# Cross attention of a decoder layer: half of the exponentials' transposes move from TensorE to DMA, the row sums into a ones column, relu into PSUM

## The reference

```
x = x + self_attention(layernorm(x))      # over groups of 4 rows at each position, 16 heads
x = x + cross_attention(layernorm(x), ctx)   # ctx: 4 x 128 x 512, 16 heads of 32
x = x + ffn(layernorm(x))                 # see below

# cross attention, per row of the batch
scores = (q @ k.T) / sqrt(32);  scores = where(mask, scores, -1e8)
attn   = softmax(scores) ;      out = attn @ v ;  out @ Wo.T + bo

# ffn
s = x @ Win + bin                         # 64 values per token
h = relu(s[..., None] * W1 + b1)          # 16 hinges per value
g = (h * W2).sum(-1) + b2
out = g @ Wout + bout
```

## Time and profile before

| | us |
|---|---|
| median of 3 runs (lowest, highest) | 1784.15 (1783.41, 1785.06) |
| the profiled execution | 1784.44 |
| its span, first to last instruction | 1782.6 |
| TensorE busy | 1685.4 (95%) |
| VectorE busy | 1514.8 (85%) |
| ScalarE busy | 1069.8 (60%) |
| GpSimd busy | 1017.6 (57%) |
| mean granted TensorE clock | 0.983 |

### The profile page before, as it was taken

The page is one execution under the profiler, slowest core; times in us unless marked ns, Lnnn a source line. Parts: engine busy times, 40 slices in busy tenths (PEclk is TensorE's granted clock), DMA queues, the critical chain, the costliest instruction groups (busy, mean ns, idle before and its releaser), DMA issues.

```text
span 1782.6 us, 37666 instructions
## 1 busy us (share of the span) xinstructions
PE 1685.4 (95%) x13824; PEld 1392.6 (78%) x13824; DVE 1514.8 (85%) x2089; ACT 1069.8 (60%) x3420; POOL 1017.6 (57%) x721
## 2 busy tenths in 40 slices
PE   6899999999999999997799999999999999999996
PEld 5678888888888888885677787778777787777874
DVE  6788888888888888787678898888988899888886
ACT  4434444444443334442767788777877788777884
POOL 3267766666666666695554464545654465544521
PEclk9999999999999999998799999999999999999998
DMA  5410111111111111044201112011111112011101
GB/s 210 128 42 25 47 48 48 47 47 47 47 47 47 47 47 47 2 107 79 68 8 51 62 62 63 25 62 62 63 38 43 62 62 69 19 62 62 39 20 54
DMA packets 72793, 98.75 MB, mean 55 GB/s; under 512 B 22208, under 2 KB 30528, under 8 KB 72640
## 3 DMA queue, kind: packets, MB, share of 16 engines
q1 hardware_dynamic: 72064, 96.63, 17.0%
q10 hardware_dynamic: 576, 0.07, 0.0%
HBM read 59.66 MB, written 37.03 MB: 54 GB/s over the span
## 4 chain that ended last, share of the span: by engine, by line
PE 28%; ACT 12%; DVE 8%; issue 4%; DVEq 0%; POOL 0%; ACTq 0%; POOLq 0%
PE ring L1464 11%; ACT prob_c L1679 10%; DVE g_sb L1794 5%; PE sc L1492 5%; PE ring L1504 3%; PE ring L1469 3%; PE ring L1549 3%; PE sc L1484 2%; PE sc L1464 1%; DVE q_first L1975 1%; ACT relu L1660 1%; DVE g_sb L1791 1%; DVE gT L1803 1%; ACT gT L1669 1%; ACT pT L1648 0%
## 5 line engine op out<-in xcount | busy, mean ns | idle before, releaser
L447 PE MATMUL qb<-wqkv,xT 128*128 128x512 f32 x2304 | 551.9, 393 | 6.1 <-DVE wqkv L1016 6.1
L447 PEld LDWEIGHTS qb<-wqkv,xT 128*128 128x128 f32 x2304 | 429.7, 189 | 93.7 <-DVE wqkv L1016 6.3
L1679 ACT ACTIVATE prob_c<-sc,ntop 128x128 f32<-128x128 f32 x1024 | 362.6, 390 | 22.1 <-DVE ntop L1821 18.7
L1410 POOL TENSOR_TENSOR rstd<-vare,half_c 128x1 f32<-128x1 f32 x64 | 35.1, 549 | 433.6 <-DVE vare L1875 433.6
L1679 ACT ACTIVATION_READ_ACCUMULATOR prob_c<-sc,ntop 128x1 f32 x1024 | 236.1, 231 | 0.0
L352 POOL TENSOR_TENSOR prod_pool<-v,prob 128x1024 f32<-128x1024 f32 x64 | 179.9, 2810 | 67.8 <-DVE prob L911 62.6
L1464 PE MATMUL ring<-wqkv,aT_c 128*128 128x512 f32 x768 | 194.5, 402 | 8.0 <-DVE aT_c L1778 7.1
L663 ACT ACTIVATE v<-qb 128x512 f32<-128x512 f32 x64 | 38.3, 598 | 259.9 <-PE qb L447 249.6
L583 PE MATMUL ob<-wout,aT 128*128 128x512 f32 x768 | 191.4, 398 | 0.8 <-DVE aT L941 0.8
L1821 DVE TENSOR_REDUCE ntop<-sc 128x4 f32<-128x512 f32 x256 | 173.3, 683 | 12.3 <-PE sc L1492 9.5
L663 ACT ACTIVATE qk<-qb 128x512 f32<-128x512 f32 x128 | 76.1, 595 | 175.8 <-PE qb L447 175.8
(11 more groups left out here) (152 smaller groups left out, 3358.5 us busy)
## 6 DMA issues: line engine op xcount, KB each, us to landing
x_tile<-in_x SPq DMA_DIRECT2D x16, 1024.0 KB, 5.2
x_scratch<-xres SPq DMA_DIRECT2D x16, 1024.0 KB, 4.6
x_tile<-x_scratch SPq DMA_DIRECT2D x16, 1024.0 KB, 5.3
out<-x SPq DMA_DIRECT2D x64, 256.0 KB, 2.0
kt<-k_scratch SPq DMA_DIRECT2D x16, 512.0 KB, 3.2
v_c<-v_scratch SPq DMA_DIRECT2D x16, 256.0 KB, 3.6
raw<-in_wqkv SPq DMA_DIRECT2D x3, 1024.0 KB, 8.9
ctx<-in_ctx SPq DMA_DIRECT2D x1, 1024.0 KB, 8.3
```

What stands on the lines that cost most here:

```text
L447: last = nc.tensor.matmul(qb[g % 4][:, :], xT[p][a][:, k, t * P:(t + 1) * P], wqkv[b][:, k, c * D:(c + 1) * D], start=(n == 0), stop=(n == ...
L1679: last = nc.scalar.activation(prob[:, h, :], sc[g][:, (h % 4) * C:(h % 4 + 1) * C], ACT.Exp, bias=ntop[:, h:h + 1], accum_out=total[:, t % ...
```

## The change

- Tiles 2 and 3 of each step are no longer transposed on TensorE. ScalarE copies the exponentials of eight heads to float16 (`part_hi`), GpSimd (tile 2) or VectorE (tile 3) writes the low part (`part_lo`), both in SBUF, and SP issues four transposing DMAs of 128 x 1024 float16 per tile (`turn`), from `p16` to `pT`. values waits for the eight heads of each half.
- The values have 34 columns per head instead of 32: a 33rd of ones in the high part, zero in the low part, and a 34th unused. The value matmuls have 33 columns, so the sum of a row comes out beside its values. The accumulator and `total` of this stage go. The result takes two ring banks.
- The ring has places of two banks for values, and one place is skipped where two would run over the end.
- relu writes into free `sc` banks (2, 3, 1; in the last two steps 2, 3) instead of SBUF buffers.
- `aT` and the pair of `g_sb` lie in unused columns of the weights' tensor. `pT` has two pairs.
- Orders: TensorE, ScalarE, VectorE, GpSimd and SP as below.

```diff
@@ slot_turns
     if t < 3:
-        return [("aT", t)] + late + [("out", t), ("wo", t), ("pv", t), ("x2T", t), ("pT", 4 * t), ("pT", 4 * t + 1)]
+        return ([("aT", t)] + late + [("out", t), ("wo", t), ("pv", t), ("x2T", t)]
+                + ([("pT", 4), ("pT", 5)] if t == 1 else []))
+    return ([("aT", 3), ("xT", 0), ("out", 3), ("xT", 1), ("wo", 3), ("xT", 2), ("xT", 3), ("pv", 3), ("x2T", 3)]
+            + [("q", m) for m in range(DK)])
+def relu_banks(n):
+    return (2, 3) if n >= TILES - 2 else (2, 3, 1)
+def ring_places():
+    place, user, n = {}, {}, 0
+    for turn in RING:
+        width = 2 if turn[1] == "pv" else 1
+        if n % 4 + width > 4:
+            n += 1
+        place[turn] = n
+        for at in range(n, n + width):
+            user[at] = turn
+        n += width
+    return place, user
@@ SP
+            def turn(j, t, part):
+                m = 2 * j + t - 2
+                heads = slice(8 * part, 8 * part + 8)
+                for h in range(2):
+                    if h == 0:
+                        wait(sp, p_hi, 2 * m + part + 1)
+                    else:
+                        wait(sp, p_lo[t - 2], 2 * j + part + 1)
+                    wait(sp, psum["pv"], 4 * j + t - 1)
+                    sp.dma_start_transpose(pT[t % 2][h][:, heads, :],
+                                           p16[h][:, heads, :].rearrange("p h c -> p (h c)")).then_inc(turned[part], 16)
             def step(j, p):
                 # load of the next x
-                if active(j - 1, "out", 3):
-                    store(j - 1, 1 - p, 3)
                 for t in range(R - 1):
                     if active(j, "out", t):
                         store(j, p, t)
+                turn(j, 2, 0); turn(j, 2, 1)
                 if has(j, 1):
                     load_ctx(j + 1, 1 - p)
+                store(j, p, 3)
+                turn(j, 3, 0); turn(j, 3, 1)
@@ GpSimd
+                def part_lo(t, part):
+                    wait(pool, p_hi, 2 * m + part + 1)
+                    wait(pool, turned[part], 32 * m)
+                    nc.gpsimd.tensor_tensor(p16[1][:, heads, :], prob[:, heads, :], p16[0][:, heads, :],
+                                            ALU.subtract).then_inc(p_lo[t - 2], 1)
...
                     residual(0)
                     residual(1)
+                part_lo(2, 0)
+                part_lo(2, 1)
                 norm2(j, 3)
@@ TensorE
 scores:
-                        wait(pe, relu_done, PAIRS * (j - 1))
+                        wait(pe, hinged, PAIRS * (j - 1))
 values:
+                        if n_dma is not None and h % 8 == 0:
+                            wait(pe, turned[h // 8], 32 * (n_dma + 1))
-                            last = nc.tensor.matmul(dst[:, head], pT[a][:, h, :], v[:, pp, b, head],
+                            last = nc.tensor.matmul(dst[:, head // 8, head % 8, :], pT[n % 2][a][:, h, :],
+                                                    v[:, pp, b, head, 0:DH + 1],
 order:
                     values(t)
                     norm2_T(t)
-                    prob_T(4 * t)
-                    prob_T(4 * t + 1)
+                    if t == 1:
+                        prob_T(4)
+                        prob_T(5)
                 scores(3)
                 attn_T(3)
                 norm_T(0)
-                prob_T(10)
-                prob_T(11)
+                ffn_out(3)
+                norm_T(1)
                 out_proj(3)
-                norm_T(1)
-                ffn_out(3)
-                values(3)
                 norm_T(2)
                 norm_T(3)
-                prob_T(12)
-                prob_T(13)
+                values(3)
                 ffn_in(j - 1)
                 norm2_T(3)
                 for m in range(DK):
                     queries(m)
-                prob_T(14)
-                prob_T(15)
@@ ScalarE
 exps:
+                    elif t == 3:
+                        wait(act, p_lo[0], 2 * j + g // 2 + 1)
+                    else:
+                        wait(act, p_lo[1], 2 * (j - 1) + g // 2 + 1)
                     for h in range(4 * g, 4 * g + 4):
                         last = nc.scalar.activation(prob[:, h, :], sc[g][:, (h % 4) * C:(h % 4 + 1) * C],
-                                                    ACT.Exp, bias=ntop[:, h:h + 1],
-                                                    accum_out=total[:, t % 2, head_of(h):head_of(h) + 1])
+                                                    ACT.Exp, bias=ntop[:, h:h + 1])
+                def part_hi(t, part):
+                    wait(act, exped, 16 * j + 4 * t + 2 * part + 2)
+                    wait(act, turned[part], 32 * m)
+                    nc.scalar.activation(p16[0][:, heads, :], prob[:, heads, :], ACT.Copy).then_inc(p_hi, 1)
 hinges:
-                        nc.scalar.activation(relu[:, i % 4, :], sc[number][:, :], ACT.Relu, bias=hinge[:, 1, i:i + 1],
+                        nc.scalar.activation(sc[banks[i % len(banks)]][:, :], sc[number][:, :], ACT.Relu,
 order of tile 3 (part_hi(2, 0) stands behind exps(2, 1)):
+                norm2_hi(2)
+                part_hi(2, 1)
+                attn_hi(3)
+                exps(3, 0)
+                norm_hi(0)
+                exps(3, 1)
+                part_hi(3, 0)
+                norm_hi(1)
+                exps(3, 2)
+                exps(3, 3)
                 norm_hi(2)
                 norm_hi(3)
-                prob_hi(j, 12)
-                prob_hi(j, 13)
+                part_hi(3, 1)
@@ VectorE
 order of tile 3:
+                norm2_lo(2)
+                tops(3, 0)
+                attn_lo(3)
+                tops(3, 1)
+                norm_lo(0)
+                tops(3, 2)
+                add_out(3)
+                tops(3, 3)
+                norm_lo(1)
+                part_lo(3, 0)
+                add_attn(3)
+                statistics(3)
                 norm_lo(2)
                 norm_lo(3)
-                prob_lo(j, 12)
-                prob_lo(j, 13)
+                normalise(3)
+                part_lo(3, 1)
```

More of the change, by code:

```diff
@@ L1223 @@
 RING = [(j, kind, i) for j in range(TILES) for kind, i in TURNS
-        if active(j, kind, i) and (j, kind, i) not in ENDING] + ENDING
-PLACE = {turn: n for n, turn in enumerate(RING)}
+        if (j, kind, i) not in ENDING] + ENDING
+def ring_places():
[9 more added lines that the diff above has]
+    return place, user
+PLACE, USER = ring_places()
 def bank_of(j, turn):
@@ L1235, in head_of, with banks_before @@
     return 4 * (slot % 4) + slot // 4
[L1238 to L1247, removed]
+def banks_before(j, turn):
+    first = PLACE[(j, *turn)]
+    found = []
+    for at in range(first, first + (2 if turn[0] == "pv" else 1)):
+        at -= 4
+        while at >= 0 and (at not in USER or not active(*USER[at])):
+            at -= 4
+        if at >= 0 and USER[at] not in found:
+            found.append(USER[at])
+    return [(kind, TURNS_OVER[kind](step, i)) for step, kind, i in found]
+CROSS_SMALL = [("kt", [P, 2, DK, C], F32R), ("fillrows", [P, C], F32R), ("v_c", [C, 2, 2, H, VW], F16),
                ("bo", [P, D], F32), ("bf", [P, D], F32), ("hinge", [P, 3, PAIRS], F32), ("bin", [P, 1], F32),
@@ L1372, in step @@
                         store(j, p, t)
+                if has(j):
+                    turn(j, 2, 0)
+                    turn(j, 2, 1)
                 if has(j, 1):
                     load_ctx(j + 1, 1 - p)
+                if active(j, "out", 3):
+                    store(j, p, 3)
+                if has(j):
+                    turn(j, 3, 0)
+                    turn(j, 3, 1)
             for p in range(2):
@@ L1379, in _ @@
             run_steps(sp, step, TILES + 1)
-            store(TILES + 1, 1, 3)
             for p in range(2):
@@ L1401, in residual @@
                     nc.gpsimd.tensor_tensor(xr[(j + 1) % 2][:, i, :], x1[:, i, :], bo[:, :], ALU.add).then_inc(res_done, 1)
+                def part_lo(t, part):
+                    if not has(j):
+                        return
+                    m = 2 * j + t - 2
+                    heads = slice(8 * part, 8 * part + 8)
+                    wait(pool, p_hi, 2 * m + part + 1)
+                    wait(pool, turned[part], 32 * m)
+                    nc.gpsimd.tensor_tensor(p16[1][:, heads, :], prob[:, heads, :], p16[0][:, heads, :],
+                                            ALU.subtract).then_inc(p_lo[t - 2], 1)
                 def norm2(j, t):
@@ L1453, in bank @@
             def bank(j, turn):
-                before = bank_before(j, turn)
-                if before:
-                    wait(pe, taken[before[0]], before[1])
+                for kind, over in banks_before(j, turn):
+                    wait(pe, taken[kind], over)
                 return ring[bank_of(j, turn)]
@@ L1734, in step @@
                     exps(0, g)
-                for t in (1, 2, 3):
+                for t in (1, 2):
                     norm2_hi(t - 1)
```

(16 more changed lines are left out.)

148 lines of the change are left out of this document (76 added, 72 removed).

## The result

The changed kernel takes 1788.87 us (median of 14 runs, 1786.14 to 1791.95), the one before 1783.70 beside it (14 runs, 1781.92 to 1785.29): ratio 1.003, interval 1.0021 to 1.0038. It is slower by 0.3%; 1756 was forecast. One of the twelve executions of the run with the ones column alone (further down) took 3279 us and is in no comparison.

What follows compares the result with a forecast made beforehand. It took TensorE's blocks and ScalarE's exponentials in turn as the bound. Gains A 0.75, B 0.15, C 0.42 in 16 steps (21.1 us), D 0.56 in 15 (8.4), last step minus 1: 28.5 off 1784.44, so 1756; range 1736 to 1815.

Steps and rivals of the forecast that it cites:

- A: Section from scores(0) to scores(1), 8.87 us before: TensorE's own work ends last at 8.1, gain 0.75 per step.
- B: Section from scores(1) to scores(2), 9.90 us before: prob_T(5) follows normalise(1), ending at 9.75, gain 0.15 per step.
- C: Section from scores(2) to scores(3), 9.92 us before: four exponentials of 0.27 follow tops(2,3), 9.5, gain 0.42 per step.
- D: Section from scores(3) to the next scores(0), 28.31 us before: 10.4 + 17.35 = 27.75, gain 0.56 in 15 steps.
- last step behind scores(3): End of the last step: values(0) follows part_lo(3,1) and its DMA, landed about 16.5 against 15.4 before: minus 1.
- D, values(3): values(3) waits for VectorE's add_attn(3) behind part_lo(3,0) of 1.8 us: it starts 10.4 after scores(3), against 7.97 before.
- D, what follows values(3): TensorE from values(3) on: 1.25 us, then 3.23 from ffn_in to the queries, then 11.3 of queries.
- D, the tail: From the queries' end to the next scores(0): hinges start at 15.4, end with the queries; 1.55 us, 2.37 before.
- GpSimd, SP and the DMAs: GpSimd's part_lo 2.6 us each; each transposing DMA takes SP's queue 1.75 to 2.2; all hidden before values(3) wants them.
- Rival 1: Transposing DMAs are slow and end the step at values(3); at 4 us each, 33 us more: 1817; chance 0.26.
- Rival 2: VectorE's part_lo costs little (1.2 us): values(3) at 9.2, 1.2 better in 15 steps, 18 us: 1738; chance 0.10.
- Rival 3: ScalarE gains nothing by the missing accumulator read (pitch 0.35), part_lo takes 2.5: 1781, no change; chance 0.12.

Runs made afterwards that it cites:

- The run without the DMAs: Kernel before plus ones column with two banks, no accumulator reads and relu in PSUM; all 16 transposes stay on TensorE: 1780.72 us, ratio 0.9987.
- add_first: Changed kernel with VectorE's part_lo(3, 0) moved behind add_attn(3): 1750.53 us, ratio 0.9817 to the kernel before.
- add_first_hinges_early: add_first with the eighth hinge moved in front of q(2)'s parts on VectorE: 1741.71 us, ratio 0.9762 to the kernel before.
- ffn_first: Changed kernel with ffn_in moved ahead of values(3) on TensorE: 1758.06 us, ratio 0.9849 to the kernel before.
- all three reorderings: Changed kernel with add_attn(3) ahead of part_lo(3, 0), ffn_in ahead of values(3), hinge 8 ahead of q(2): 1736.37 us, ratio 0.973 to the kernel before.

## Why the prediction was wrong

Forecast 1756, measured 1786.14 in the profiled execution: 30 us more, and slower than before where a gain was forecast. By the starts of the score blocks, summed over all steps, measured against forecast:

| part | forecast against before | measured | off by |
|---|---|---|---|
| A, 16 steps | -12.0 | -10.0 | 2.0 |
| B, 16 | -2.4 | +2.8 | 5.2 |
| C, 16 | -6.7 | -8.3 | -1.6 |
| D, 15 | -8.4 | +15.9 | 24.3 |
| last step behind scores(3) | +1.0 | +3.0 | 2.0 |

The rows leave 1.8 us, which lie ahead of the stage.

- **A.** Right: 8.15 for 8.1, and the pitch 0.27 as taken. TensorE's own work ends last there. Most of the 2.0 are two sections 0.9 longer, in which the clock was down.
- **B.** Wrong in sign, small; the mechanism was right and its size was not. The step said that prob_T(5) would follow normalise(1), 9.3 + 0.44 (by its row, 1148.73 less 1139.54, the first is 9.19). It does follow it, by the code and by time: normalise(1) ends 9.38 into B (1202.92), prob_T(5) starts 0.15 later (1203.07) and scores(2) 0.56 after that, so B is 10.09. The run without the DMAs has the same B and the same wait, so it belongs to the ones column and its two banks, and the run with the ones column alone shows that this edit is worth nothing by itself.
- **C.** Right: 9.5.
- **D, values(3).** Right: 10.4 forecast, 10.5 measured; part_lo 1.8 forecast, 1.92 to 1.95 there. 1.8 was the middle between two rows and not worked out, so that it held so well is in part luck. The one part_lo with nothing on GpSimd beside it took 1.22 (last step of add_first).
- **D, what follows values(3): the step that failed first.** "Behind values(3): 1.25, 3.23, 11.3" took ffn_in at the price that it has when TensorE is kept busy. The text's own 7.8 (TensorE alone) and 10.4 make a stand of 2.6 us, and it knew of a long stand and of the clock, but only as a sign that would show it wrong; the sum had no term for it. Summed over the 14 steps, D is 10.5 us above the 28.55 of the steps at full clock, and the A behind one of them is 0.9 longer: 11.4. Filling the stand gives 11.4 back.
- **D, the tail: the second.** "Hinges end with the queries; the tail is 1.55" makes 12.85 from the queries to scores(0); 13.56 to 13.65 is what the steps at full clock show, 0.75 more, some 11 us. The step looked at the start of the hinges and at their sum. It did not look at the order in VectorE's queue, where the last hinge stands behind the low part of q(2), which has to wait for TensorE: that holds the time at 13.2 even where gate_lo takes 0.69. Moved in front, 13.04 is left, of which 0.2 is a wait for the last query's low part.
- **D, the tail: the third.** The other 0.4 of the 0.75 is gate_lo, 1.07 to 1.16 in these steps. GpSimd's norm of the next step runs beside it: it starts 22.4 to 23.1 behind scores(3), 15.8 before the change, because the load of the next x stands behind tile 3's transposes in SP's queue. The prediction gave that shift (23 rather than 16) and put it at "nothing", as nobody waits for the norm; it did not ask what the norm would then run beside.
- **The first two steps.** D in steps 0 and 1 was 25.90 and 27.71 before, not 28.31, and the forecast took 0.56 off all alike; measured are 26.82 and 29.09. That is some 2 us of the 24.3.
- **GpSimd, SP and the DMAs.** Right in what the transposes need for themselves: the queue takes 1.23 (1.75 to 2.2 taken), GpSimd's part_lo 2.14 (2.6 taken), and TensorE waits for none of them. Rival 1 falls: even at 8.63, values(3) is released by VectorE. Only in the last step was a second half released by a DMA, with waits of 0.71 in add_first and 1.18 in add_first_hinges_early. Rival 2 was not what happened (its 9.2 and 18 us go with a part_lo of 0.6; by the same sum 1.2 gives 9.8 and 9 us), but add_first shows what an earlier values(3) brings: it starts 1.87 earlier there. Rival 3 falls by the pitch.
- **The hinges.** The price 0.75 was right throughout. The run with relu in PSUM alone shows that this was the one part of the change that gained by itself (0.29%). It also bears out the shared port, which the prediction took from the Trainium skill, SBUF — State Buffer, Who interferes with whom: with one operand in PSUM, two of VectorE's hinges took 1.60 instead of 2.79, and GpSimd's operation of the norm beside it, 1.22 to 1.49 before, takes 1.04.

Without the fallen clock a step would be 56.3 (8.15 + 10.09 + 9.5 + 28.55), 0.7 better than before where 1.9 was forecast. What stays open is why the clock held in three of 14 steps behind the same stand; the traces show no difference in front of them, and I did not try to tell.

## What to carry to other kernels

When a change takes work from TensorE and adds a wait, price the wait and what TensorE does right behind it at the lower clock; if the wait can't go, put work that is due anyway into it. Follow the queue of the engine that holds the last wait instruction by instruction: a line placed in front of the operation that frees a bank cost 38 us here, and a hinge behind a subtraction 0.6% more. When a change shifts an operation that nobody waits for, ask what it will now run beside: gate_lo became 0.4 us longer by the norm here. Test a change's parts alone, since here one gained 0.3%, one gained nothing, and the third was good only behind a reordering.

## What the runs showed of the hardware

- Behind a stand of 2.65 to 2.71 us TensorE's clock fell in 11 of 14 steps, and with the stand filled in none. In ffn_first it fell behind waits of 1.91, 1.98 and 2.14 us and not behind one of 2.01, and with all three reorderings once behind 1.64. Stands of 0.8 us were never followed by it in the 14 steps of add_first_hinges_early.
- A transposing DMA of 128 x 1024 float16 from SBUF to SBUF takes 1.23 us of SP's queue and 3.4 to land (median; 3.0 to 5.8), while in the stretch shown above the 16 DMA engines move 195 GB/s.
- Without the accumulator read a 128-column exponential follows the one before by 0.27 us, with it by 0.35.
- A VectorE subtraction of 1024 columns, float32 minus float16 into float16, took 1.22 us with GpSimd idle and 1.83 to 1.95 beside GpSimd. In add_first it took 1.35, and it was GpSimd's residual beside it that grew, to 2.28 from 1.27 for the one in front.
- A VectorE subtraction of 512 columns with both operands in SBUF took 0.69 us alone and up to 1.56 beside GpSimd's norm (gate_lo in ffn_first).
